# Value products of a half step in one block instead of two, with four buffers of turned probabilities

## The chip, the cores and the metric

The kernel runs on one NeuronCore of a Trainium2 chip. The metric is the device time of one launch in microseconds (us), median of the runs.

## The reference, cut to what matters

Two transformer layers on x of shape (64, 128, 256): 64 sequences of 128 tokens, width 256, float32. Each layer is a cross attention to a context of the same shape, then a mixture of experts. The change touches the two cross attentions only:

```
# layer 0: dilated attention; with 128 tokens per sequence its three branches are causal softmax
# attentions over all, every second and every fourth token, mixed by their log-sum-exp
x = x + L0_xattn(layernorm(x), ctx, ctx)
x = x + L0_ffn(layernorm(x))            # attention and MLP, each a mixture of 8 experts
# layer 1: plain causal attention
q, k, v = (n @ Wq + bq), (ctx @ Wk + bk), (ctx @ Wv + bv)      # 16 heads of 16
scores  = q k^T / 4, masked above the diagonal
x = x + softmax(scores) v @ Wo + bo
x = x + L1_ffn(layernorm(x))            # 8 experts, the best one of each token
```

## The kernel before

The program is a chain of stages: set-up, attention of layer 0 (its first scores begin 37 us into the span), the attention and the MLP of mixtures of layer 0, attention of layer 1 (from 2245 to 2790 us), routed experts. Both attentions are one function, `attention` (L270), called twice. The three branches of layer 0 become one softmax: what differs is added to the scores as a mask.

**Tiling.** The 64 sequences go two by two: 32 pairs per attention. A pair has two half steps, one for each sequence (s = 0, 1). In a half step the 16 heads are four units of four heads. A unit's scores, 128 queries by 4 x 128 keys, fill one PSUM bank (banks 0 to 3). So there are 64 half steps in each attention, 128 in all. `pairs` (L325) writes out the first 10 pairs (layer 0) or 2 pairs (layer 1) and the last 4, and runs the ones between in a hardware loop of two pairs per turn: 18 pairs in layer 0 and 26 in layer 1.

**One unit's way.** TensorE writes mask and scores of all four units at once (`score`, L419: 8 mask matmuls at L428, 16 products at L437). VectorE takes the row maximum of each unit (`row_max`, L632). ScalarE takes the exponentials, head by head, with their sums (`exps`, L555; lines L562). TensorE turns the unit's four probability matrices (`turn_p`, L442; transposes at L447) into bank 4 (units 0, 2, 3) or bank 0 (unit 1). VectorE copies them to SBUF, into `probsT` (`keep_p`, L638; copy at L642). TensorE multiplies them with the values (`times_v`, L450; L460, four column strips of the array at a time) into bank 5. The inverse of the sums is made and spread (`invert` on VectorE, `spread` on GpSimd), turned into the other half of bank 5 (`turn_recip`, L464), and `keep_o` (L650) copies bank 5 out.

**Order.** Each engine's order is written out by hand in its own `step`; the engines meet through semaphores that count. TensorE's half step is: score, turn unit 3 of the half step before, project the next pair's values (s = 0) or keys (s = 1), `times_v` of units 2 and 3 of the half step before, turn unit 0, `turn_recip`, project queries (s = 0) or the output (s = 1), turn units 1 and 2, with s = 0 turn the normalized x (`turn_n`, L370), `times_v` of units 0 and 1. VectorE's is: row maximum 0, keep unit 3 of before, row maxima 1 to 3, keep unit 0, keep_o, with s = 0 `keep_v` (L619), keep units 1 and 2, with s = 1 `residual`, `invert`, and with s = 0 `stats` and `rest_n` (L615). In the first pairs of layer 0 VectorE also measures x (`measure`, L727) between them. ScalarE's is four times `exps`, then with s = 0 `keep_q` and `round_n` (L537), with s = 1 `keep_k`, `norm` and, at the next pair's start, `round_c`.

**Waits that matter here.** `probsT` has two buffers, unit k uses k % 2: so `keep_p(k)` waits until `times_v(k - 2)` is done (`pv_done`, L641). The first mask matmul of `score` waits until unit 1's turned probabilities have left bank 0 (`pT_ready`, L427), and the mask matmul of unit u until the exponentials of unit u of the half step before are done (`exp_done`, L425). `rest_n` waits for `round_n`, and `project_k` for `rest_n` (`nlo_ready`, L382).

Of the kernel before, what the change touches and what calls it, by code (L numbers as in the profile page):

```python
# [26 lines left out]
P = 128  # L27
# [6 lines left out]
UH = 4  # L34
UNITS = H // UH
# [17 lines left out]
def wait(eng, sem, value):  # L53

    if isinstance(value, int) and value <= 0:
        return
    eng.wait_ge(sem, value)


def is_(index, value):  # L60

    return isinstance(index, int) and index == value
# [9 lines left out]
class Signals:  # L72
# [6 lines left out]
    def sem(self, name):  # L79
        self.all.append(self.stack.enter_context(self.nc.semaphore(name)))  # L80
        return self.all[-1]
# [188 lines left out]
def attention(nc, S, L, ctx_dram, W, bias, counted, load_next, signals, first, next_norms, next_table, x_dram=None):  # L270

    NP = S.n_seq // 2
# [3 lines left out]
    UP = 2 * UNITS  # L276
    rest_k16 = S.rest_count_k16 if counted else S.rest_k16
    with ExitStack() as mem:
        def sb(name, shape, dt=F32):
            return mem.enter_context(nc.sbuf_tensor(f"{L}_{name}", shape, dt))  # L280
# [8 lines left out]
        kT = sb("kT", [P, 2, KT, 2 * P])  # L289
        v_pad = sb("v_pad", [P, 2, 2, 2, 2 * UH, 32])  # L290
        probs = sb("probs", [P, UNITS, UH, P])
        probsT = sb("probsT", [P, 2, UH, P])
        neg_max = sb("neg_max", [P, UNITS, UH])
        sums, recip = sb("sums", [P, 2, KT, UH, 2]), sb("recip", [P, 2, KT, UH * 2])
        recip_wide = sb("recip_wide", [P, 2, KT, UH * 2 * D])
# [4 lines left out]
        pT_ps = [S.bank[n].rearrange("p (h k) -> p h k", h=UH) for n in (4, 0, 4, 4)]  # L300
# [14 lines left out]
        pT_made, pT_ready, pv_done, o_kept = sem("pT_made"), sem("pT_ready"), sem("pv_done"), sem("o_kept")  # L315
# [20 lines left out]
        with nc.Block() as block:  # L336
# [32 lines left out]
            def _(pe):  # L369
# [72 lines left out]
                def turn_p(p, k):  # L442
                    wait(pe, exp_done, UP * p + k + 1)
                    if k % UNITS != 1:
                        wait(pe, pT_ready, UP * p + k - (k % UNITS == 2))
                    for i in range(UH):
                        last = pe.transpose(pT_ps[k % UNITS][:, i, :], probs[:, k % UNITS, i, :], S.ident[:])  # L447
                    last.then_inc(pT_made, 1)

                def times_v(p, b, k):  # L450

                    s, u = divmod(k, UNITS)
                    m, e = divmod(u, 2)
                    wait(pe, pT_ready, UP * p + k + 1)
                    if u == 0:
                        wait(pe, o_kept, 2 * p + s)
                    if k == 0:
                        pe.wait_ge(v_ready, p + 1)
                    for i in range(UH):
                        last = pe.matmul(o_ps[32 * i:32 * (i + 1), 0, m, :], v_pad[:, b, s, e, UH * m + i, :],  # L460
                                         probsT[:, k % 2, i, :], start=u == 0, stop=True, skip_group_check=True)
                    last.then_inc(pv_done, 1)

                def turn_recip(p, s):  # L464
# [6 lines left out]
                def step(p, b):  # L471
                    for s in range(2):
                        before = (p, b, UNITS) if s else (p - 1, 1 - b, UP)
                        exists = s == 1 or not is_(p, 0)
                        score(p, b, s)
                        if exists:
                            turn_p(before[0], before[2] - 1)
                        if s == 0 and more(p, 1):
                            project_v(p + 1, 1 - b)
                        if s == 1 and more(p, 2):  # L480
                            project_k(p + 2, b)
                        if exists:
                            times_v(before[0], before[1], before[2] - 2)
                            times_v(before[0], before[1], before[2] - 1)
                        turn_p(p, UNITS * s)
                        if exists:
                            turn_recip(before[0], before[2] // UNITS - 1)
                        for half in range(2):
                            if s == 0 and more(p, 1):
                                project_q(p + 1, half)  # L490
                            if s == 1 and not is_(p, 0):
                                project_o(p - 1, half)
                        turn_p(p, UNITS * s + 1)
                        turn_p(p, UNITS * s + 2)
                        if s == 0 and more(p, 2):
                            turn_n(p + 2)
                        for u in range(2):
                            times_v(p, b, UNITS * s + u)

                turn_n(0)  # L500
                busy(pe, S, 8)
# [8 lines left out]
                project_k(1, 1)  # L510
                pairs(pe, step)
                turn_p(NP - 1, UP - 1)
                times_v(NP - 1, 1, UP - 2)
                times_v(NP - 1, 1, UP - 1)
                turn_recip(NP - 1, 1)
                for s in range(2):
                    project_o(NP - 1, s)
# [96 lines left out]
            def _(dve):  # L614
# [23 lines left out]
                def keep_p(p, k):  # L638

                    dve.wait_ge(pT_made, UP * p + k + 1)  # L640
                    wait(dve, pv_done, UP * p + k - 1)  # L641
                    dve.tensor_copy(probsT[:, k % 2], pT_ps[k % UNITS]).then_inc(pT_ready, 1)  # L642

                def invert(p, s):

# [1774 lines left out]
def program(nc, a, out):  # L2420

    with ExitStack() as mem:
# [66 lines left out]
        with ExitStack() as own:  # L2489
            W = Named()  # L2490
            W.hi, W.lo = weights(own, "W0", [P, 4, KT, C])
            signals = Signals(nc)
            attention(nc, S, "L0", a["ctx"], W, B["L0_xattn"], True, load_weights(1), signals, True, 2, ACT.Exp, a)
# [57 lines left out]
```

## Time and profile before

| | |
|---|---|
| median of 3 runs | 3059.33 us (3059.03 to 3063.7) |
| span of the profiled execution, first to last instruction | 3021.6 us |
| TensorE busy in it | 2857.8 us |
| VectorE busy in it | 2286.3 us |
| ScalarE busy in it | 1877.8 us |
| GpSimd busy in it | 1564.7 us |
| mean granted TensorE clock | 0.974 of full |

The profile is of one execution. It gives that execution's span and no other time of it; the span is 37.7 us under the median of the timed runs, which also holds what lies before the first and after the last instruction. Engines: PE is TensorE's matmuls, PEld its weight loads, DVE is VectorE, ACT is ScalarE, POOL is GpSimd. L460 is line 460 of the kernel. A time in brackets at the end of a row of the timeline is how long the engine sat idle before it, and behind the arrow what ended that ("issue": nothing that the profile shows).

### The profile page before, as it was taken

The page shows a single profiled execution, that of the slowest core. Times are in us where ns is not written, and L with a number is a line of the kernel's source. Part 1 is how long each engine was busy: PE and PEld are TensorE (multiplying, and loading weights), DVE is VectorE, ACT ScalarE, POOL GpSimd, SP SyncE. Part 2 cuts the span into 40 slices and gives each one's busy share as a digit, 9 for nine tenths or more (in the row PEclk, how much of TensorE's full clock was granted, in tenths as well). Part 3 has the DMA queues.
Part 4 walks back from the last instruction along what each step waited for, and adds up shares of the span by engine and source line. Part 5 has one row for each costly group of instructions (what it writes and reads, how often), then busy time and mean ns, then how long its engine had stood idle before and what let it go on. Part 6 is the DMA issues. An engine that isn't in the chain of part 4 may idle for free. (4 is left out here: it accounts for less than half of the span.)

```text
span 3021.6 us, 85335 instructions
## 1 busy us (share of the span) xinstructions
PE 2857.8 (95%) x26943; PEld 2563.3 (85%) x26944; DVE 2286.3 (76%) x6211; ACT 1877.8 (62%) x6970; POOL 1564.7 (52%) x1816
## 2 busy tenths in 40 slices
PE   6999999889999999997999999999989999998778
PEld 5878888689999999996999999999988888886556
DVE  6988888877777777776777777777768888888745
ACT  5888888755555555555344444444458888887735
POOL 3565656466666666665322222222226666654556
PEclk9999999999999999998999999999999999999779
DMA  6000000010000000000000000000010000000245
GB/s 222 16 19 15 17 14 14 2 62 11 10 10 10 10 11 12 10 10 25 25 11 10 10 10 10 10 10 10 5 47 18 17 14 14 17 14 2 93 140 150
DMA packets 56235, 86.43 MB, mean 29 GB/s; under 512 B 6944, under 2 KB 42785, under 8 KB 55458
## 3 DMA queue, kind: packets, MB, share of 16 engines
q1 hardware_dynamic: 49284, 66.47, 7.0%
q0 software_dynamic: 6528, 16.92, 1.5%
q8 instruction: 75, 1.23, 0.2%
q10 hardware_dynamic: 288, 1.31, 0.1%
q14 instruction: 60, 0.49, 0.1%
HBM read 57.25 MB, written 28.48 MB: 28 GB/s over the span
## 5 line engine op out<-in xcount | busy, mean ns | idle before, releaser
L562 ACT ACTIVATE L_probs<-bank,L_neg_max 128x128 f32<-128x128 f32 x2048 | 716.8, 403 | 150.4 <-DVE L_neg_max L636 149.9
L562 ACT ACTIVATION_READ_ACCUMULATOR L_probs<-bank,L_neg_max 128x1 f32 x2048 | 497.8, 243 | 0.0
L642 DVE COPY L_probsT<-bank 128x512 f32<-128x512 f32 x512 | 353.0, 689 | 136.6 <-PE bank L460 81.5
L1719 ACT ACTIVATE M_inter<-bank 128x512 f32<-128x512 f32 x256 | 153.3, 599 | 438.8 <-PE bank L69 387.9
L67 PE MATMUL bank<-W_hi,M_nT_hi 128*128 128x384 f32 (+1 forms) x1024 | 370.2, 362 | 8.3 <-DVE M_qkv L1345 4.4
L636 DVE TENSOR_REDUCE L_neg_max<-bank 128x4 f32<-128x512 f32 x512 | 327.6, 682 | 30.7 <-PE bank L437 30.6
L69 PE MATMUL bank<-W_lo,M_nT_hi 128*128 128x384 f32 (+1 forms) x1024 | 346.8, 339 | 0.0
L68 PE MATMUL bank<-W_hi,M_nT_lo 128*128 128x384 f32 (+1 forms) x1024 | 346.6, 338 | 0.0
L447 PE MATMUL bank<-constants,L_probs 128*128 128x128 f32 x2048 | 327.3, 284 | 12.9 <-ACT L_probs L562 10.1
L1778 DVE TENSOR_TENSOR M_inter_lo<-M_inter,M_inter_hi 128x512 fp32r<-128x512 f32 x256 | 207.1, 809 | 168.5 <-ACT M_inter_hi L1720 158.2
L67 PE MATMUL bank<-W_hi,M_inter_hi 128*128 128x256 f32 x1024 | 290.5, 284 | 11.8 <-DVE M_inter_lo L1778 11.0
L67 PE MATMUL bank<-M_nT_hi,W_hi 128*128 128x256 f32 x1024 | 296.8, 290 | 0.0
L447 PEld LDWEIGHTS bank<-constants,L_probs 128*128 128x128 f32 x2048 | 220.7, 141 | 82.7 <-ACT L_probs L562 66.6
L69 PE MATMUL bank<-M_nT_lo,W_hi 128*128 128x256 f32 x1024 | 290.4, 284 | 0.0
L68 PE MATMUL bank<-M_nT_hi,W_lo 128*128 128x256 f32 x1024 | 289.5, 283 | 0.0
L68 PE MATMUL bank<-W_hi,M_inter_lo 128*128 128x256 f32 x1024 | 287.7, 281 | 0.0
L69 PE MATMUL bank<-W_lo,M_inter_hi 128*128 128x256 f32 x1024 | 287.5, 281 | 0.0
L1875 POOL TENSOR_TENSOR M_gate_rnorm<-M_gate_squared,constants 128x2 f32<-128x2 f32 x32 | 24.4, 763 | 487.2 <-DVE M_gate_squared L1765 487.2
L818 POOL TENSOR_TENSOR L_o<-L_o_raw 128x256 f32<-128x256 f32 x128 | 93.3, 729 | 289.6 <-DVE L_o_raw L656 282.5
L67 PEld LDWEIGHTS bank<-W_hi,M_nT_hi 128*128 128x128 f32 x1024 | 193.6, 189 | 37.3 <-DVE M_qkv L1345 8.7
L1206 ACT ACTIVATE M_qkv_part<-bank,M_rw 128x384 f32<-128x384 f32 x192 | 111.5, 581 | 157.9 <-PE bank L69 157.8
L67 PEld LDWEIGHTS bank<-W_hi,M_inter_hi 128*128 128x128 f32 x1024 | 193.8, 189 | 18.2 <-issue 16.6
(334 smaller groups left out, 9144.7 us busy)
## 6 DMA issues: line engine op xcount, KB each, us to landing
L_ctx_in<-in_ctx SPq DMA_DIRECT2D x64, 256.0 KB, 2.6
M_tile<-M_sorted SPq DMA_DIRECT2D x72, 130.0 KB, 2.3
x_all<-in_x SPq DMA_DIRECT2D x8, 1024.0 KB, 10.5
raw_weights<-in_weights SPq DMA_DIRECT2D x2, 4096.0 KB, 15.6
hs<-M_hs SPq DMA_DIRECT2D x64, 128.0 KB, 1.7
M_hs<-hs SPq DMA_DIRECT2D x32, 256.0 KB, 2.6
M_sorted<-M_fill SPq DMA_DIRECT2D x16, 130.0 KB, 2.1
raw_weights<-in_weights SPq DMA_DIRECT2D x1, 2048.0 KB, 8.0
```

The source lines that it names most:

```text
L67: pe.matmul(out, left[0], right[0], start=first, stop=False)
L68: pe.matmul(out, left[1], right[0], start=False, stop=False)
L69: return pe.matmul(out, left[0], right[1], start=False, stop=last)
L447: last = pe.transpose(pT_ps[k % UNITS][:, i, :], probs[:, k % UNITS, i, :], S.ident[:])
L562: last = act.activation(probs[:, k % UNITS, i, :], score_bank[u][:, i, :], ACT.Exp, bias=neg_max[:, u, i:i + 1], scale=-1.0, accum_out=sum ...
L636: dve.tensor_reduce(neg_max[:, u, :], score_bank[u], AX.X, ALU.min).then_inc(max_ready, 1)
L642: dve.tensor_copy(probsT[:, k % 2], pT_ps[k % UNITS]).then_inc(pT_ready, 1)
L818: pool.tensor_tensor(o_sb[:], o_raw[:, s, 0, :], o_raw[:, s, 1, :], ALU.mult)
L1206: act.activation(qkv_part[:, e // 2 - 1, :], q_bank[1], ACT.Copy, scale=rw[:, b, 0, e:e + 1]).then_inc(M.odd_read, 1)
L1719: act.activation(inter[:, e % 2], up_bank[e % 2], ACT.Gelu).then_inc(M.inter_ready, 1)
L1778: dve.tensor_tensor(iT[1][:, e % 2].rearrange("p k t -> p (k t)"), inter[:, e % 2], iT[0][:, e % 2].rearrange("p k t -> p (k t)").bitcast( ...
L1875: pool.tensor_tensor(T.rnorm[:], T.squared[:], S.minus_half[:, 0:T.n], ALU.pow).then_inc(M.rooted, 1)
```

## The change

`probsT` gets four buffers instead of two, one for each unit. `times_v` of units 0 and 1 moves from the end of its half step into the block that already stands in the next one, so that this block holds units 0 to 3 in order. After the last pair it does so too. `keep_p(k)` waits for `times_v(k - 4)` instead of `times_v(k - 2)`. Number and shape of all instructions stay the same.

```diff
-        probsT = sb("probsT", [P, 2, UH, P])
+        probsT = sb("probsT", [P, UNITS, UH, P])
...
                         last = pe.matmul(o_ps[32 * i:32 * (i + 1), 0, m, :], v_pad[:, b, s, e, UH * m + i, :],
-                                         probsT[:, k % 2, i, :], start=u == 0, stop=True, skip_group_check=True)
+                                         probsT[:, u, i, :], start=u == 0, stop=True, skip_group_check=True)
...
                         if exists:
-                            times_v(before[0], before[1], before[2] - 2)
-                            times_v(before[0], before[1], before[2] - 1)
+                            for u in range(UNITS, 0, -1):
+                                times_v(before[0], before[1], before[2] - u)
                         turn_p(p, UNITS * s)
...
                         if s == 0 and more(p, 2):
                             turn_n(p + 2)
-                        for u in range(2):
-                            times_v(p, b, UNITS * s + u)
...
                 turn_p(NP - 1, UP - 1)
-                times_v(NP - 1, 1, UP - 2)
-                times_v(NP - 1, 1, UP - 1)
+                for u in range(UNITS, 0, -1):
+                    times_v(NP - 1, 1, UP - u)
...
                     dve.wait_ge(pT_made, UP * p + k + 1)
-                    wait(dve, pv_done, UP * p + k - 1)
-                    dve.tensor_copy(probsT[:, k % 2], pT_ps[k % UNITS]).then_inc(pT_ready, 1)
+                    wait(dve, pv_done, UP * p + k - UNITS + 1)
+                    dve.tensor_copy(probsT[:, k % UNITS], pT_ps[k % UNITS]).then_inc(pT_ready, 1)
```

## Rows read from the trace of the kernel before

**Rows 1.** The page: busy time, and the granted TensorE clock in 40 slices.
```profile
PE 2857.8 (95%) x26943; PEld 2563.3 (85%) x26944; DVE 2286.3 (76%) x6211; ACT 1877.8 (62%) x6970; POOL 1564.7 (52%) x1816
...
PEclk9999999999999999998999999999999999999779
```

**Rows 2.** Waits, whole span: waiter, cause, total us, times, longest.
```profile
DVE L_probsT L642 <- PE bank L460: 81.5, 128, 1.2
```

**Rows 3.** Timeline of ScalarE, one pair of layer 0's loop.
```profile
513.42 0.29 ACT L562 ACTIVATION_READ_ACCUMULATOR L_probs<-bank,L_neg_max 128x1 f32 x1
...
514.23 0.70 ACT L540 ACTIVATE L_nT_hi<-bank 128x512 fp32r<-128x512 f32 x1
516.64 0.37 ACT L562 ACTIVATE L_probs<-bank,L_neg_max 128x128 f32<-128x128 f32 x1 [1.71 <-DVE L_neg_max L636]
...
522.04 0.29 ACT L562 ACTIVATION_READ_ACCUMULATOR L_probs<-bank,L_neg_max 128x1 f32 x1
```

**Rows 4.** Timeline of VectorE, the same pair.
```profile
510.40 0.69 DVE L642 COPY L_probsT<-bank 128x512 f32<-128x512 f32 x1 [0.18 <-PE bank L447]
...
512.40 0.69 DVE L642 COPY L_probsT<-bank 128x512 f32<-128x512 f32 x1
513.96 0.69 DVE L642 COPY L_probsT<-bank 128x512 f32<-128x512 f32 x1 [0.87 <-PE bank L460]
...
514.73 0.69 DVE L670 BATCH_NORM_STATS2 stats<-x_all  x2
515.33 0.68 DVE L617 TENSOR_TENSOR L_nT_lo<-bank,L_nT_hi 128x512 fp32r<-128x512 f32 x1
515.92 0.68 DVE L636 TENSOR_REDUCE L_neg_max<-bank 128x4 f32<-128x512 f32 x1
```

**Rows 5.** Timeline of TensorE's weight loads, the same pair.
```profile
509.04 0.38 PEld L460 LDWEIGHTS bank<-L_probsT,L_v_pad 128*32 128x32 f32 x16
509.62 0.42 PEld L447 LDWEIGHTS bank<-constants,L_probs 128*128 128x128 f32 x4 [0.20 <-ACT L_probs L562]
...
511.66 0.46 PEld L447 LDWEIGHTS bank<-constants,L_probs 128*128 128x128 f32 x4
512.37 0.42 PEld L447 LDWEIGHTS bank<-constants,L_probs 128*128 128x128 f32 x4 [0.25 <-ACT L_probs L562]
...
513.39 0.38 PEld L460 LDWEIGHTS bank<-L_probsT,L_v_pad 128*32 128x32 f32 x16 [0.17 <-issue]
513.97 0.12 PEld L428 LDWEIGHTS bank<-constants 32*128 32x128 bf16 x8 [0.20 <-ACT L_probs L562]
...
516.12 0.19 PEld L67 LDWEIGHTS bank<-L_cT_hi,W_hi 128*128 128x128 f32 x1 [0.30 <-issue]
...
520.32 0.45 PEld L447 LDWEIGHTS bank<-constants,L_probs 128*128 128x128 f32 x4
```

**Rows 6.** Timeline of TensorE's matmuls, the same pair.
```profile
514.41 1.06 PE L437 MATMUL bank<-L_kT,L_q_half 32*128 32x128 f32 x32
```

**Rows 7.** Timeline of VectorE, first pair of layer 1.
```profile
2253.80 0.69 DVE L617 TENSOR_TENSOR L_nT_lo<-bank,L_nT_hi 128x512 fp32r<-128x512 f32 x1 [0.15 <-ACT L_nT_hi L540]
2254.41 0.68 DVE L636 TENSOR_REDUCE L_neg_max<-bank 128x4 f32<-128x512 f32 x1
```

**Rows 8.** Timeline of ScalarE, first pair of layer 1.
```profile
2252.26 0.30 ACT L562 ACTIVATION_READ_ACCUMULATOR L_probs<-bank,L_neg_max 128x1 f32 x1
```

**Rows 9.** Waits of the weight loads in 240 to 540 us.
```profile
PEld bank L428 <- issue: 6.0, 18, 0.5
```

**Rows 10.** Busy time by windows: length, busy by engine, granted clock, DMA.
```profile
53.36:60.19 6.83, 6.43 (x58) 4.67 (x62) 5.48 (x14) 6.47 (x30) 2.64 (x4) 0.50 0.10 38
...
240.00:540.00 300.00, 296.23 (x4138) 249.46 (x4140) 253.93 (x500) 263.63 (x1285) 181.21 (x231) 1.00 0.05 15
```

**Rows 11.** Timeline of VectorE, third pair of layer 0.
```profile
84.50 0.69 DVE L642 COPY L_probsT<-bank 128x512 f32<-128x512 f32 x1 [0.88 <-PE bank L460]
...
87.12 0.68 DVE L636 TENSOR_REDUCE L_neg_max<-bank 128x4 f32<-128x512 f32 x1
```

## The prediction, made before the changed kernel ran

> **What bounds the kernel now.** The page comes first. TensorE is busy 95% of the span [rows 1], so one would look for TensorE work that goes away. The change removes none; it only reorders. So the question is whether TensorE sets the pace in the two attentions, or a ring of waits through all engines does. The list of waits gives the lead: VectorE's copy of turned probabilities waits for a value product 128 times, once in every half step, 81.5 us in total [rows 2]. Whether that costs anything is read from the timelines of one pair.
>
> In them the last exponential of half step s = 0 ends at 513.42 + 0.29 = 513.71 and the first of the next half step starts at 516.64, after ScalarE sat idle for 1.71 us; it ends with the last one at 522.04 + 0.29 = 522.33 [rows 3]. From end to end that is 8.62 us: 2.93 from the last exponential to the first, 5.69 of exponentials. ScalarE waits in the first part, so what fills these 2.93 us is the bound. The first exponential follows row maximum 0, started at 515.92, by 0.72. That one stands at the end of a VectorE chain without any gap: copy of unit 2 at 513.96, reciprocal, statistics at 514.73, `rest_n` at 515.33, row maximum [rows 4]. The copy had been idle 0.87 us, and its releaser is `times_v` (L460). The scores themselves were not late: their first load is at 513.97 [rows 5] and their last product ends at 514.41 + 1.06 = 515.47 [rows 6], so a `score` takes 1.50 and was complete 0.45 before the row maximum begins. So in s = 0 the ring is: turn unit 2, `turn_n`, `times_v(0)` at 513.39 [rows 5], copy of unit 2, the VectorE chain, row maximum, exponentials. The wait for `times_v(k - 2)` is what the change takes away.
>
> In s = 1 the VectorE chain has no `stats` and no `rest_n`, and the next score is gated by the last exponential. There the ring has no `times_v` in it, save after the loop's branch (below).
>
> **The change, part by part.**
>
> *TensorE, s = 0.* The block of value products starts at 509.04 as before. With two units it took 0.58 to the next load, 509.62 [rows 5]. With four: at least 0.58 + 0.38 (the loads of two more units) = 0.96, at most two whole blocks, 1.16. I take 1.05. Unit 0 is then turned at 510.09 instead of 509.62 (its exponentials were done just before 509.62). From there to the turn of unit 1 are 2.04 us of matmuls (509.62 to 511.66 [rows 5]): 512.13. The turn of unit 2 then follows in 0.46 to 0.71 (the loads alone; 511.66 to 512.37, where 0.25 was waiting for ScalarE): 512.59 to 512.84. The 0.25 of waiting is the cover that takes up half of the delay. At the end of the half step 0.58 of value products (513.39 to 513.97) is gone.
>
> *VectorE, s = 0.* A copy starts about 0.78 after its turn starts (509.62 to 510.40 [rows 4, 5]). Unit 0: 510.87. Then `keep_o` and `keep_v` run as before, and the copy of unit 1 follows 2.00 later (510.40 to 512.40): 512.87. The copy of unit 2 no longer waits for a product; its turn allows it at 513.37 to 513.62 and VectorE is free at 512.87 + 0.61 = 513.48. So it starts between 513.48 and 513.62, instead of 513.96. What is late next? Reciprocal and statistics (0.77 from the copy to the statistics, 0.60 from these to `rest_n`) leave VectorE free for `rest_n` at 514.85 to 514.99. `rest_n` also needs `round_n` of ScalarE, which ends at 514.93 [rows 3]. This floor shows in the first pair of layer 1, where no statistics stand in the chain: `rest_n` starts at 2253.80, idle before it and released by ScalarE, 1.24 after the last exponential (2252.26 + 0.30), and the row maximum 0.61 later [rows 7, 8]. Here that gives `rest_n` at 514.96, row maximum at 515.57, first exponential at 516.29: 0.35 earlier than 516.64. The new limit is ScalarE's `round_n`, and the chain of VectorE beside it within 0.1.
>
> Score must not be late: it may now start when its first wait and the last exponential allow, about 513.71 + 0.05, and be complete at 515.27, 0.30 before the row maximum wants it. Its wait for the copy of unit 1 ends at 512.87 + 0.69 = 513.56. Behind that wait on TensorE stand only the scores.
>
> *s = 1.* `rest_n` ends 0.37 earlier, and `project_k` waits for it (516.12 [rows 5]), so it starts 0.37 earlier; the longer block costs 0.47; the turn of unit 1 is at 520.32 + 0.10 = 520.42, its copy at +0.74 = 521.16 to 521.85. The last exponential moves from 522.33 to 521.97. So score's first wait ends 0.1 before its last one: no loss, but no more than 0.1 of cover. Nothing is gained here in a plain half step. After the loop's branch there is something: of the 18 waits "issue" before score in 300 us, 6.0 us in all with a longest of 0.5 [rows 9], if nine are about 0.2, as the one before score in [rows 5], the other nine are 0.47 on average, one per turn of the loop. With the value products gone TensorE reaches the branch early. Bounds are 0 and 0.3 for each; I take 0.15.
>
> *Other queues.* `keep_o` comes about 0.5 later, and with it GpSimd's `normalize`; GpSimd is busy 181 of 300 us [rows 10], and its results are wanted in the next half step, so I cost it at nothing; without that cover it would cost what exceeds some 3 us. ScalarE and the DMA queues issue what they issued. After the last pair two more units (about 0.4 us) stand before the last product, but run while TensorE waits for the copy of unit 3 (0.69): nothing.
>
> *Sum.* Loop pairs: 18 + 26 = 44, times 0.35 = 15.4. Loop branches: 8 + 12 = 20, times 0.15 = 3.0. Pairs written out with the same chain (10th of layer 0, 29th and 30th of each attention): 5 x 0.35 = 1.8. Pairs 3 to 7 of layer 0: their chain from the copy of unit 2 to the row maximum has the measurements in it too, is unbroken and 2.62 long (84.50 to 87.12, 0.88 idle before it [rows 11]), so ScalarE's floor is not reached and the whole shift of the copy counts, 513.96 - 513.48 = 0.48: 5 x 0.48 = 2.4. Pairs 1, 2 and 8 of layer 0, same chain with other work: I take 0.4 each, 1.2. The first two and last two pairs of layer 1 and the last two of layer 0 have ScalarE's floor or a shorter chain: 0. Together 23.8 us. The profiled span would go from 3021.6 to 2997.8; the median is 37.7 above the span, which I keep: 3059.3 - 23.8 = 3035.5, say **3035**.
>
> **The rivals.**
>
> *A, part of it is given back.* The copies of units 1 and 2 come later than worked out, because the block or the two turns take longer. Each 0.1 beyond the 0.1 of cover costs 0.1 in s = 0 and as much in s = 1. With 0.2 too late in both: 64 x (0.1 + 0.1) = 13 of the 24, 3048. For it: the cover is thin in both half steps. Against: both are worked out with their upper ends (1.16, 0.71) and still hold nearly all.
>
> *B, no change.* The copy's idle time is no cause but a consequence, and the first exponential is held by something else to 2.93 after the last: 3059. For it: an engine that is busy 95%. Against: the pair of [rows 7, 8] has 2.57 there (0.72 more than 2254.41 - 2252.56), with the same scores and ScalarE work.
>
> *C, slower: score behind the copy of unit 1.* Today 0.58 of value products lie between the turns and score; they cover the copy out of bank 0. Without them score waits for it directly, with all matmuls behind it. Place: the first mask matmul. If the copy of unit 1 is late by L against the times above, s = 1 loses L - 0.1 and s = 0, whose copy of unit 2 follows it, changes by L - 0.48: slower from L of about 0.3. Priced at 0.7, one more VectorE operation before it: 64 x (0.6 + 0.2) = 51, less the 3 of the branches, 3107.
>
> *D, slower: the clock.* TensorE would now pause briefly before each score. The granted clock is 1.00 (2.4 GHz) in the loop with TensorE busy 296 of 300 us, and 0.50 (1.2 GHz) at 53 to 60 us, where the start-up left TensorE waiting [rows 10]. If half the length of that stretch, 3.4 us, ran at 1.2 GHz in each pair, its matmuls would take up to 1.7 us more: 64 x 1.7 = 109, 3144 with the gain. Against: pauses of 0.2 to 0.4 in 8.3 us are as long as those that the loop has already. The Trainium skill, "TensorE: Matmul & The Clock Gate", section "A second HAM failure mode: psum-queue depth-cycling", tells of a kernel whose short pauses between groups of matmuls made the clock go up and down; the loop's 1.00 shows nothing of it so far.
>
> *E, more: TensorE is the bound after all.* Then the change saves what stands around the moved block, the 0.17 before it and the 0.20 behind it [rows 5], in each half step: 128 x 0.37 = 47, 3012. The Trainium skill, "TensorEngine Tiling (Array Packing)", section "Key Properties", says that a change of tiling mode drains the engine, which would be these gaps; the trace agrees, as they stand where the array goes from whole to column strips and from these to row strips. Against: ScalarE is idle for 1.71 and TensorE waits for ScalarE (0.25) in the same half step.
>
> **How the numbers follow.** Forecast 0.70, A 0.12, B 0.08, C 0.04, D 0.03, E 0.03. What a measurement of this kernel tells from no change is about 0.2%, 6 us. Faster: forecast, A and E, 0.85. Same: B, 0.08. Slower: C and D, 0.07. Range: the forecast's terms with branches at 0.3 and chains at 0.40 give 20 x 0.3 + 49 x 0.40 + 3.6 = 29 us, 3030; with some to spare 3027. Upwards to A and a little beyond it, 3052; with B, C, D and most of E outside it leaves out somewhat under 2 in 10.
>
> **What would show it.** In the profile after: the waits of L642 for L460 gone; first exponential of s = 1 at 2.57 after the last one of s = 0, `rest_n` idle before it and released by L540; the block of L460 with 32 loads once per half step, turn of unit 0 about 1.05 after its start; the way from the last exponential of s = 1 to the first of s = 0 unchanged in plain half steps. Wrong, if the copy of unit 2 starts later than 0.12 before the last exponential ends, if score's first load comes after the last exponential of s = 1, or if the clock of the loops is under 0.98.

## The result, and the profile after

| | before | after |
|---|---|---|
| median of 4 runs | 3059.61 us (3059.03 to 3063.7) | 3036.01 us (3034.01 to 3038.49) |
| span of the profiled execution | 3021.6 us | 3031.9 us |
| time of that run | not given | 3034.01 us |
| attention of layer 0, layer 1 | 541.1, 528.2 us | 526.3, 516.4 us |
| last stage (routed experts) | 240.8 us | 276.4 us |
| the rest between the attentions | 1665.0 us | 1666.2 us |

The ratio is 0.9921, with a 95% interval of 0.9907 to 0.9934: 23.6 us faster, where 3035 was forecast. An attention is counted here from the last exponential of its first half step to that of its last one. The two together went from 1069.3 to 1042.6, 26.7 us less.

The two spans can't be compared as they stand: the profiled span after is longer, though the kernel is faster. No chip is on record for the profile and the times before, but two things say that they come from different ones: the last stage takes 235 to 242 us in every trace of one chip and 274 to 280 us in every trace of another, whichever kernel runs (the last section), and the kernel before takes 3025 us on the first and 3064 us on the second. The profile before is like the first in both, the times before are like the second. All comparisons of traces below leave that stage out.

First the waits, whole span, of after (waiter, cause, us in total, times, longest). `keep_p`'s copy is L640 now, two lines up.

```profile
ACT L_probs L560 <- DVE L_neg_max L634: 123.0, 120, 4.6
DVE L_probsT L640 <- PE bank L447: 108.6, 185, 1.1
PEld bank L428 <- ACT L_probs L560: 27.7, 76, 0.7
PEld bank L428 <- DVE L_probsT L640: 25.6, 44, 0.6
```

The wait for L460 [rows 2] is gone. ScalarE's wait for the row maximum is down from 149.9 to 123.0, by 26.9, about the gain in the attentions (26.7). VectorE's copies now wait for the turns instead (108.6 us against 49.8), which is not a loss by itself: they wait because they are early. TensorE's weight loads now pause before `score` (L428), for the exponentials or for the copy of unit 1.

One pair of layer 0's loop, as in [rows 3 to 5]. The weight loads of after:

```profile
495.31 0.81 PEld L460 LDWEIGHTS bank<-L_probsT,L_v_pad 128*32 128x32 f32 x32
496.32 0.42 PEld L447 LDWEIGHTS bank<-constants,L_probs 128*128 128x128 f32 x4 [0.20 <-issue]
...
498.37 0.90 PEld L447 LDWEIGHTS bank<-constants,L_probs 128*128 128x128 f32 x8
499.31 0.42 PEld L376 LDWEIGHTS bank<-constants,L_normed 128*128 128x128 f32 x4
500.00 0.24 PEld L428 LDWEIGHTS bank<-constants 32*128 32x128 bf16 x8 [0.28 <-ACT L_probs L560]
```

The block has 32 loads, and the turn of unit 0 starts 1.01 after it (estimate 1.05). The two turns of units 1 and 2 now stand without a gap, and `score` follows `turn_n` directly, 0.02 after the last exponential (next fence but one). VectorE:

```profile
497.11 0.69 DVE L640 COPY L_probsT<-bank 128x512 f32<-128x512 f32 x1 [0.62 <-PE bank L447]
...
499.20 1.29 DVE L640 COPY L_probsT<-bank 128x512 f32<-128x512 f32 x2
500.40 0.24 DVE L646 RECIPROCAL L_recip<-L_sums 128x16 f32<-128x16 f32 x1
500.56 0.69 DVE L668 BATCH_NORM_STATS2 stats<-x_all  x2
501.23 0.69 DVE L615 TENSOR_TENSOR L_nT_lo<-bank,L_nT_hi 128x512 fp32r<-128x512 f32 x1
501.84 0.68 DVE L634 TENSOR_REDUCE L_neg_max<-bank 128x4 f32<-128x512 f32 x1
```

The copies of units 1 and 2 are one run (x2, 0.6 apart), so unit 2's starts at 499.8, 0.18 before the last exponential ends; before, it started 0.25 after it. And ScalarE:

```profile
499.69 0.29 ACT L560 ACTIVATION_READ_ACCUMULATOR L_probs<-bank,L_neg_max 128x1 f32 x1
...
500.50 0.70 ACT L538 ACTIVATE L_nT_hi<-bank 128x512 fp32r<-128x512 f32 x1
502.56 0.37 ACT L560 ACTIVATE L_probs<-bank,L_neg_max 128x128 f32<-128x128 f32 x1 [1.36 <-DVE L_neg_max L634]
...
507.95 0.29 ACT L560 ACTIVATION_READ_ACCUMULATOR L_probs<-bank,L_neg_max 128x1 f32 x1
```

From last exponential to first it is 502.56 - 499.98 = 2.58 us, where it was 2.93 [rows 3], and from last to last 508.24 - 499.98 = 8.26, where it was 8.62. The clock, from the page, and a window in the loop of layer 0 (length, busy time by engine, granted clock, DMA):

```profile
PE 2831.6 (93%) x26944; PEld 2595.6 (86%) x26944; DVE 2283.2 (75%) x6211; ACT 1877.9 (62%) x6970; POOL 1563.8 (52%) x1816
...
PEclk9999999899999999997999999999999999998598
```

```profile
240.00:520.00 280.00, 272.81 (x3956) 246.96 (x3958) 243.19 (x479) 252.75 (x1231) 174.52 (x222) 1.00 0.05 15
```

The pauses before `score` left the granted clock at 1.00 (2.4 GHz). TensorE's busy share in the loop fell from 99% (296.23 of 300 [rows 10]) to 97% (272.81 of 280): its matmuls stand idle for 7.2 us before `score` in this window, 5.6 of them for the copy of unit 1 (16 times, 0.35 each). The kernel got faster with a less busy TensorE.

### The profile page after: what moved, and what is told of

It is laid out like the page before. It is cut to its first block and busy times, and to the rows that moved or that the text cites. A ratio compares the mean times of both kernels' runs of the same rounds, so it can differ in the third digit from the quotient of the medians.

```text
span 3031.9 us, 85376 instructions
## 1 busy us (share of the span) xinstructions
PE 2831.6 (93%) x26944; PEld 2595.6 (86%) x26944; DVE 2283.2 (75%) x6211; ACT 1877.9 (62%) x6970; POOL 1563.8 (52%) x1816
## 5 line engine op out<-in xcount | busy, mean ns | idle before, releaser
L560 ACT ACTIVATE L_probs<-bank,L_neg_max 128x128 f32<-128x128 f32 x2048 | 716.7, 402 | 123.9 <-DVE L_neg_max L634 123.0
L640 DVE COPY L_probsT<-bank 128x512 f32<-128x512 f32 x512 | 341.9, 687 | 110.3 <-PE bank L447 108.6
L447 PE MATMUL bank<-constants,L_probs 128*128 128x128 f32 x2048 | 304.5, 281 | 12.2 <-ACT L_probs L560 10.1
L447 PEld LDWEIGHTS bank<-constants,L_probs 128*128 128x128 f32 x2048 | 222.8, 141 | 57.5 <-issue 23.6
```

The costliest lines, as they stand in the source:

```text
L560: last = act.activation(probs[:, k % UNITS, i, :], score_bank[u][:, i, :], ACT.Exp, bias=neg_max[:, u, i:i + 1], scale=-1.0, accum_out=sum ...
L640: dve.tensor_copy(probsT[:, k % UNITS], pT_ps[k % UNITS]).then_inc(pT_ready, 1)
```

## The experiments

Two sets, each on one chip with its own runs of the kernel before: on the first its median was 3024.97 us (3021.51 to 3031.12, 17 runs), on the second 3063.84 us (3059.36 to 3072.05, 13 runs). Times across the sets are compared as ratios only. Periods (from the last exponential of one half step to that of the next) and the times after the last exponential of the half step before are medians over twenty pairs of layer 1's loop, unless a row is shown.

### e1_after_again: the changed kernel, no edit

> The changed kernel once more, for its loops and for the last stage. Open: in the two profiles the attentions became 26.7 us shorter, yet the span grew by 10.3, since the last stage (routed experts) took 35.6 us more after the change; the timed runs became 23.6 faster. Theory: the last stage varies from execution to execution, whatever the attentions do, and the profile of before caught a short one; then the ratio here is again 0.992 with its interval below 0.995, and the attentions' loop pairs take 16.43 us. Rival: the change lengthens the last stage; then the last stage stays above 270 us here in every execution and under 245 us in those of the kernel before.

Measured: 2996.64 us (2992.6 to 3003.59), ratio 0.9911 (0.9896 to 0.9926). The gain of the result came again, with 28.3 us in the medians and 23.9 in the attentions of the traces (1069.3 to 1045.4). The last stage takes 235.8 us with the changed kernel here, so the rival falls; what else it depends on is taken up in e5. This run is the reference for the next three.

### e2_buffers_only: four buffers, old order

From the kernel before:

```diff
-        probsT = sb("probsT", [P, 2, UH, P])
+        probsT = sb("probsT", [P, UNITS, UH, P])
...
-                                         probsT[:, k % 2, i, :], ...
+                                         probsT[:, u, i, :], ...
...
-                    wait(dve, pv_done, UP * p + k - 1)
-                    dve.tensor_copy(probsT[:, k % 2], pT_ps[k % UNITS])
+                    wait(dve, pv_done, UP * p + k - UNITS + 1)
+                    dve.tensor_copy(probsT[:, k % UNITS], pT_ps[k % UNITS])
```

> Four buffers of turned probabilities, with TensorE's order as before (value products of units 0 and 1 at the end of their half step). Theory: the gain comes from the copy of unit 2, which no longer waits for a value product, so that the next row maximum stands 1.86 after the last exponential instead of 2.21; score may be 0.3 later than in the changed kernel without harm. So half steps s = 1 of the loops take 8.26 as in the changed kernel, only the part of the branch is missing: about 19 to 21 us under the kernel before, 3040. Rival: the gain needs the block to move (TensorE's order, fewer changes of shape); then this one is within 6 us of the kernel before.

Measured: 3003.63 us (2995.58 to 3007.35), ratio 0.9926 (0.9912 to 0.9941). So 21.3 of the 28.3 us of e1 are there without any instruction having moved. The intervals of the two overlap; the attentions of the two traces are within 0.5 us of each other (1045.9 and 1045.4), while the last stage, which neither edit touches, takes 241.5 us here and 235.8 in e1. So the 7 us between the medians are no measure of the move. Weight loads, VectorE and ScalarE of one pair:

```profile
2567.94 0.38 PEld L460 LDWEIGHTS bank<-L_probsT,L_v_pad 128*32 128x32 f32 x16 [0.16 <-issue]
2568.51 0.12 PEld L428 LDWEIGHTS bank<-constants 32*128 32x128 bf16 x8 [0.20 <-ACT L_probs L562]
```

```profile
2566.99 1.40 DVE L642 COPY L_probsT<-bank 128x512 f32<-128x512 f32 x2
2570.12 0.68 DVE L636 TENSOR_REDUCE L_neg_max<-bank 128x4 f32<-128x512 f32 x1
```

```profile
2567.96 0.30 ACT L562 ACTIVATION_READ_ACCUMULATOR L_probs<-bank,L_neg_max 128x1 f32 x1
2570.84 0.37 ACT L562 ACTIVATE L_probs<-bank,L_neg_max 128x128 f32<-128x128 f32 x1 [1.36 <-DVE L_neg_max L636]
```

The value products still stand in front of `score`, which still starts 0.25 after the last exponential (2568.51 - 2568.26), as before. All the same the row maximum comes at 1.86 and the first exponential at 2.58, as in the changed kernel. So in s = 1 the copy's wait was the whole loss, and the late `score` none. What the move itself gives stands at the loop's branches: the two hardware loops took 742.0 us before (303.5 + 438.5), 727.1 here and 724.2 in e1. That is 14.9 us for the buffers (15.4 forecast) and 2.9 for the branches (3.0 forecast).

The move also costs something. Pairs 3 to 7 of layer 0 take 87.2 us before, 82.4 here and 84.6 in e1. There the chain from the copies to the row maximum sets the pace, and behind the longer block the copy of unit 0 starts 0.3 later: 2.97 before the last exponential ends in pair 5 of the result's trace, 3.27 here. So over both attentions the four buffers alone are as good as the whole change: most of the 2.9 us that the move gives at the branches is lost again in these five pairs (2.2).

### e3_two_blocks: the value products in two blocks of the next half step

From the changed kernel, in TensorE's step:

```diff
+                        if exists:
+                            for u in range(UNITS, UNITS - 2, -1):
+                                times_v(before[0], before[1], before[2] - u)
                         if s == 1 and more(p, 2):
                             project_k(p + 2, b)
                         if exists:
-                            for u in range(UNITS, 0, -1):
+                            for u in range(UNITS - 2, 0, -1):
                                 times_v(before[0], before[1], before[2] - u)
```

The same happens with s = 0 around the projection of the values. Nothing but TensorE's order changes.

> The changed kernel, but its block of four units is cut in two in the next half step: units 0 and 1 right after the turn of unit 3, units 2 and 3 after the projection. It puts one more change of array shape (about 0.2 us each way) back in each half step, 128 times, and leaves all waits alone. Theory: TensorE has slack in both half steps (about 0.2), and nearly all of it is used; loss against the changed kernel 0 to 10 us. Rival, TensorE is the bound: 0.37 x 128 = 47 us are lost, which is slower than before the change.

Measured: 3024.64 us (3019.75 to 3027.51), ratio 0.9994 (0.9985 to 1.0003). The whole gain is lost, far outside what I expected; the rival's size is nearer, but too large as well. Weight loads of one pair, then the first load of a `score` of s = 0, then ScalarE:

```profile
2584.72 0.38 PEld L460 LDWEIGHTS bank<-L_probsT,L_v_pad 128*32 128x32 f32 x16
2585.30 0.42 PEld L447 LDWEIGHTS bank<-constants,L_probs 128*128 128x128 f32 x4 [0.20 <-issue]
...
2588.98 0.24 PEld L428 LDWEIGHTS bank<-constants 32*128 32x128 bf16 x8 [0.28 <-ACT L_probs L563]
...
2591.12 0.38 PEld L460 LDWEIGHTS bank<-L_probsT,L_v_pad 128*32 128x32 f32 x16 [0.17 <-issue]
2591.70 0.19 PEld L67 LDWEIGHTS bank<-L_cT_hi,W_hi 128*128 128x128 f32 x1 [0.20 <-issue]
```

```profile
2563.49 0.20 PEld L428 LDWEIGHTS bank<-constants 32*128 32x128 bf16 x8 [0.58 <-DVE L_probsT L643]
```

```profile
2588.35 0.30 ACT L563 ACTIVATION_READ_ACCUMULATOR L_probs<-bank,L_neg_max 128x1 f32 x1
2591.45 0.37 ACT L563 ACTIVATE L_probs<-bank,L_neg_max 128x128 f32<-128x128 f32 x1 [1.58 <-DVE L_neg_max L637]
```

Each block stands between a gap of 0.13 to 0.17 and one of 0.20. One more block in each half step is 2 x (0.33 to 0.37) = 0.66 to 0.74 us more on TensorE in a pair. The periods grew from 8.18 and 8.28 (e1) to 8.45 and 8.49, by 0.48 together. So TensorE had about 0.2 of room in a pair, 0.1 in a half step, and all beyond it is paid in full. `score` now starts 0.33 after the last exponential (2588.98 - 2588.65), and the first exponential follows at 2.80. The changed kernel was thus close to a second bound, TensorE's own sequence, which is the thin cover that the prediction named in both half steps; I had taken it for thicker when I wrote this expectation. In s = 0 it is not TensorE alone: `score` starts 0.23 after the last exponential (2563.49 - 2563.26), when the copy of unit 1 lets it (the single row above), so that the bound there is TensorE up to the turn of unit 1 and then its copy, rival C's wait. With the copy's wait gone, the gaps of one more block at this place are no longer free. (e2 has two groups per half step as well, but its second one stands directly before `score`, which it makes 0.25 late in s = 1 without making the row maximum late.)

### e4_floor: the two things that hold `rest_n`, earlier

From the changed kernel. ScalarE splits x before it keeps the queries, and VectorE's statistics go before the copies of units 0 to 2:

```diff
# ScalarE's step, s == 0
+                        round_n(p + 2)
                         keep_q(p + 1)
-                        round_n(p + 2)
# VectorE's step
+                        if s == 0 and not (is_(p, 0) or is_(p, 1)):
+                            stats(p - 2)
                         keep_p(p, UNITS * s)
...
                         invert(p, s)
-                        if s == 0 and not (is_(p, 0) or is_(p, 1)):
-                            stats(p - 2)
```

> The changed kernel with the floor that was named as the new limit taken away: ScalarE rounds the next pair's normalized x before it keeps the queries, and VectorE takes the statistics of x ahead of the copy of unit 0, where it has been idle, instead of between the copy of unit 2 and the row maximum. Theory: the row maximum of s = 1 then follows the scores at about 1.60 after the last exponential instead of 1.86, half steps s = 1 take 8.00 to 8.05 instead of 8.26, 64 x 0.21 to 0.26 = 13 to 17 us under the changed kernel, 3020 to 3023. Rival: TensorE is the limit by now (its score is complete at 1.55 to 1.70); then half of that, 3028 or so, or nothing.

Measured: 2986.53 us (2986.17 to 2986.81), ratio 0.9872 (0.9857 to 0.9886), 10.1 us under e1. Weight loads, VectorE and ScalarE of one pair:

```profile
2559.18 0.24 PEld L428 LDWEIGHTS bank<-constants 32*128 32x128 bf16 x8 [0.26 <-issue]
```

```profile
2560.85 0.69 DVE L634 TENSOR_REDUCE L_neg_max<-bank 128x4 f32<-128x512 f32 x1 [0.25 <-PE bank L437]
```

```profile
2558.90 0.30 ACT L560 ACTIVATION_READ_ACCUMULATOR L_probs<-bank,L_neg_max 128x1 f32 x1
2561.58 0.37 ACT L560 ACTIVATE L_probs<-bank,L_neg_max 128x128 f32<-128x128 f32 x1 [0.97 <-DVE L_neg_max L634]
```

The row maximum now waits for the scores (L437) instead of the VectorE chain, and the first exponential is at 2.38 instead of 2.57. So the floor was `rest_n`, as the theory says, and lifting it gives 0.19 in s = 1. The rest of the way to what I expected is lost to TensorE: `score` there is released by nothing that the profile shows, it just comes when TensorE gets to it, and s = 0 went from 8.18 to 8.23. So the loops gave 6.0 us (724.2 to 718.2), where 44 x 0.21 to 0.26 = 9 to 11 were expected. Another 4.0 came from the first ten pairs (166.1 to 162.0). The two moves were not tried apart, so the share of each is open. This is the fastest kernel of this set.

### e5_before_again: the kernel before, no edit

> The kernel before once more, for the spans of its executions and for its last stage. The first profile of the changed kernel had 276 us after the last exponential of layer 1, three later ones on another chip 236 to 242, among them one of the same changed kernel; the profile of before had 241. Theory: the last stage differs between chips, not between kernels, and only about 2 us lie around a span, so the 37.7 us that the prediction put around it were mostly that difference. Then span and time differ by about 2 here, and the last stage is within 5 us of that of the other kernels of this job. Rival: the time around the span is about 38 for this kernel.

Measured: 3063.43 us (3054.59 to 3068.91), ratio 1.000 (0.999 to 1.001). It gives a trace of the kernel before on the second chip: attentions 539.5 and 528.8 us, within 1.6 of the first trace, and a last stage of 274.4 instead of 240.8. The profiled run takes 3054.59 us for a span of 3052.6, so 2.0 us lie around the span and the rival's 38 falls. The last stages of e6, e7 and e8 take 277.9, 280.0 and 277.8 us, one of them 0.6 further off than the 5 us expected.

### e6_wait_order: ScalarE waits for the row maximum last

From the changed kernel, in `exps`; the other two waits (for the turned probabilities and for the inverse; the inverse is ready 0.36 us before the row maximum starts in both traces below) now stand ahead of it:

```diff
-                    act.wait_ge(max_ready, UP * p + k + 1)
...
+                    act.wait_ge(max_ready, UP * p + k + 1)
```

> The changed kernel, but ScalarE waits for the row maximum after its other waits, not ahead of them. Between the start of row maximum 0 and the first exponential lie 0.89 us in the loops with s = 0, and 0.72 elsewhere; if the 0.16 is ScalarE working out its later waits, it goes, and half steps s = 0 of the loops could fall from 8.17 to 8.01. Theory: TensorE's own ring (score, turn of unit 3, projection, block, two turns, projection) is about 8.1 long by now, so they fall by 0.03 to 0.07 only, 1 to 3 us in all. Rival: TensorE is not near its limit; 44 x 0.16 = 7 us.

Measured: 3035.55 us (3031.37 to 3038.84), ratio 0.9902 (0.9881 to 0.9923), which can't be told from 0.9911. The traces show more. Row maximum 0 and first exponential of one half step s = 0, first the changed kernel:

```profile
394.85 0.69 DVE L634 TENSOR_REDUCE L_neg_max<-bank 128x4 f32<-128x512 f32 x1 [0.35 <-PE bank L437]
```

```profile
395.73 0.37 ACT L560 ACTIVATE L_probs<-bank,L_neg_max 128x128 f32<-128x128 f32 x1 [0.25 <-DVE L_neg_max L634]
```

And with the edit:

```profile
396.22 0.69 DVE L634 TENSOR_REDUCE L_neg_max<-bank 128x4 f32<-128x512 f32 x1 [0.35 <-PE bank L437]
```

```profile
396.95 0.37 ACT L560 ACTIVATE L_probs<-bank,L_neg_max 128x128 f32<-128x128 f32 x1
```

From row maximum to exponential it is 0.88 in the one and 0.73 in the other. In s = 1 of the loops, where ScalarE has been idle for over a microsecond, it is 0.71 to 0.72 with either order. Nearness of the waits to the row maximum does not explain this, though: in pairs 29 and 30 of both attentions, which are written out, ScalarE is idle still more briefly in s = 0 (0.09 to 0.11 us, for 0.25 in the loops), yet the changed kernel has 0.72 to 0.73 there, and with the edit it is 0.80 to 0.82, in s = 1 as well. The period of s = 0 fell from 8.17 to 8.02; that of s = 1 rose from 8.26 to 8.34, since its `score` now starts 0.17 after the last exponential. A pair takes 16.36 where it took 16.43: half is given back, where TensorE comes later to `score`. The loops together went from 722.8 to 719.6 us, the written-out pairs from 319.8 to 325.1 (0.1 more in most of their half steps, and two falls of the clock, see below), so that the attentions as a whole are 2.1 us longer with the edit.

### e7_floor_and_order: e4 and e6 together

> The last two edits together: ScalarE's rounding ahead of the queries, statistics moved into VectorE's idle time, and the row maximum awaited last. Every wait off TensorE would then allow half steps of 8.00. Theory, TensorE's ring bounds: 8.10 to 8.15 in all loop half steps, 0 to 3 us under the kernel with the first two edits alone, that is 38 to 41 under the kernel before. Rival: 8.00 in all of them, 10 to 13 us under it.

Measured: 3027.02 us (3025.50 to 3029.94), ratio 0.9874 (0.9855 to 0.9893), where e4 alone had 0.9872. A pair takes 16.31 us here and 16.32 in e4. Two edits that shorten two different waits add up to what the better one gives: the sign of a common bound that neither touches. `score` of s = 1 starts 0.17 after the last exponential, where e4 had 0.01 to 0.02 before it; that of s = 0 still waits 0.58 for the copy of unit 1.

### e8_less_tensor_work: e7 with less for TensorE to do

The projections of the queries and of the output leave out one of the three products that make an accurate one (the low part of the weights or of the output times the high part); of twelve matmuls in each, four go:

```diff
-                        last = mm3(pe, q_ps[:, m, :], ...
+                        last = mm2(pe, q_ps[:, m, :], ...
...
-                        last = mm3(pe, y_ps[:, s, :], ...
+                        last = mm2(pe, y_ps[:, s, :], ...
```

> The kernel of the run before this one, with one of the three products of each projected query and output tile left out (the low-order term; 4 of 12 matmuls of 256 columns in each half step, 0.12 us each, 0.48 us). It leaves out part of the computation. Theory: TensorE bounds the loops now, so that with 0.48 less they fall to the floor of the other engines, 8.00 to 8.03: 10 to 18 us under the run before it. Rival: something else holds them at 8.15 (a copy, ScalarE); then this one takes as long.

Measured: 3018.92 us (3018.13 to 3021.54), ratio 0.9851 (0.9832 to 0.9869), 8.1 us under e7. The traces show 4.7 less in the attentions (1033.9 to 1029.3): 5.9 less in the loops and 1.3 more in the pairs written out. The rest lies in stages that the edit does not touch. Either figure is less than the 10 to 18 expected. TensorE is a bound of e7, then, but not all of it. In s = 0 the period is 8.02 (8.06 in e7), and the first load of `score` comes 0.48 before the last exponential ends. In s = 1 it is 8.16 (8.25 in e7), and the weight loads show another wait. The last row is from the matmuls:

```profile
2566.50 1.02 PEld L453 LDWEIGHTS bank<-constants,L_probs 128*128 128x128 f32 x8
2567.91 0.42 PEld L382 LDWEIGHTS bank<-constants,L_normed 128*128 128x128 f32 x4 [0.39 <-issue]
2568.51 0.24 PEld L434 LDWEIGHTS bank<-constants 32*128 32x128 bf16 x8 [0.18 <-ACT L_probs L566]
```

```profile
2567.94 0.63 PE L382 MATMUL bank<-constants,L_normed 128*128 128x128 f32 x4 [0.18 <-DVE L_v_pad L630]
```

```profile
2566.92 0.88 DVE L630 TENSOR_TENSOR L_v_pad<-bank,rows 128x128 f32<-128x128 f32 x4
```

`turn_n` (L382 here) sat 0.39 idle. In the code it waits for `keep_v`, whose four operations VectorE ends at about 2567.8, 0.1 before `turn_n` starts. For the loads the profile names "issue", for the matmuls behind them `keep_v` (L630). That this wait is what still holds s = 1 is argued; no kernel here moved `keep_v` to show it.

## Why the prediction was right

**The bound.** A ring of waits, not TensorE's busy share: shown by e2, which takes nothing from TensorE and gives 14.9 us in the loops. Rival B (no change) falls.

**The copy of unit 2** was to start 0.09 to 0.23 before the last exponential; it starts 0.18 before. Block to turn of unit 0: 1.01, for 1.05.

**The new floor.** First exponential at 2.58 for 2.57 to 2.58, row maximum at 1.86. The period of s = 1 went from 8.61 to 8.26, 0.35 as forecast; e4 shows that `rest_n` is what holds it. One sign that I named did not show: `rest_n` is not idle before it. ScalarE's `round_n` ends at 501.20 and VectorE's statistics at 501.25, and `rest_n` starts at 501.23, so the two are level. I had them within 0.1 of each other and took `round_n` as the later; it changes nothing in the sum, but it is why e4 moved both.

**The cover of `score`.** The way from s = 1 to s = 0 was to stay as it was, with 0.1 of cover, and in half steps without a branch it does (first exponential at 2.47 before and after). Before it TensorE now waits 0.58 for the copy of unit 1:

```profile
393.20 0.22 PEld L428 LDWEIGHTS bank<-constants 32*128 32x128 bf16 x8 [0.58 <-DVE L_probsT L640]
```

That is rival C's wait, at its place. It ends 0.06 before the last exponential (393.26), so it costs nothing here; a lateness of some 0.1 more would begin to be paid. Rival A, the same lateness in small, did not come either.

**The terms of the sum.** Both loops: 18.4 forecast; 19.2 measured by the result's trace, 17.8 by e1's. Last four pairs of both attentions: 1.4 forecast, 1.1 measured (each 65.22 to 64.68). First ten pairs of layer 0: 4.0 forecast, 6.4 measured (172.3 to 165.9), but only 4.2 between the two later traces (e5's 170.3 to e1's 166.1). The difference is not the change's. Half step s = 0 of pair 9 went from 9.27 to 8.00 in the result's traces, since in the profile before the granted clock fell to 0.50 (1.2 GHz) just ahead of it; in e5, the same kernel, it did not, and the half step took 8.02. Of the ten traces three have the fall, with 9.02 to 9.27 in this half step, and seven do not, with 8.00 to 8.10. The stretch in both (length, busy time by engine, granted clock, DMA):

```profile
179.70:183.00 3.30, 3.30 (x18) 3.30 (x17) 1.17 (x2) 3.30 (x21) 0.57 (x1) 0.50 0.01 2
```

```profile
179.70:183.00 3.30, 3.19 (x53) 2.45 (x55) 1.67 (x3) 3.30 (x19) 2.14 (x3) 1.00 0.01 2
```

Pair 2 has another such difference (9.67 and 8.83 in s = 0 of the two traces before, with the clock at 0.50 for 6.8 us in the one and 3.4 in the other). Without these two half steps the first ten pairs gave 4.9 us in either comparison, 0.9 more than forecast. Pairs 3 to 7 gave 0.54 each on average for 0.48 (2.7 for 2.4), pairs 1, 2 and 8 together 0.8 for 1.2. Pair 9 had been left out of the sum, though its s = 1 has the plain chain (8.61 to 8.26, 0.35). And pair 10 gave 0.76 in s = 0 (9.29 to 8.53; 9.25 to 8.49 in e5 and e1), where I had forecast nothing: the turn of the inverse there waits for GpSimd, first before, then after.

```profile
198.75 0.20 PEld L468 LDWEIGHTS bank<-constants,L_recip_wide 128*128 128x128 f32 x2 [1.45 <-POOL L_recip_wide L808]
```

```profile
193.16 0.20 PEld L468 LDWEIGHTS bank<-constants,L_recip_wide 128*128 128x128 f32 x2 [0.53 <-POOL L_recip_wide L806]
```

The prediction had put everything on GpSimd at nothing, which holds in the loop and not here.

Together 23.8 were forecast in the attentions, 26.7 measured (23.9 by e1 against the trace before, 22.9 by e1 against e5), and 23.6 in the medians. In e1's set the medians give 28.3. So the sum is right by its terms, but that it hit the measured median to 1 us is partly luck.

**The account around the span was wrong.** I took 37.7 us to lie around the profiled span. In every run since, a profiled run's time is 2 us above its own span (3034.01 and 3031.9 after). Most of the rest is the last stage of the profile before, which is 34 us shorter than in e5. Only the difference of 23.8 went into the forecast, so the error cancelled. In a change to the last stage it need not have.

**The clock** (rival D) stayed at 1.00 in the loop, where the rival wanted 0.50 for part of each pair. Pauses of 0.28 and 0.58 us before `score`, one in each half step on the weight loads and 0.35 of the second on the matmuls, did nothing to it. The Trainium skill, "TensorE: Matmul & The Clock Gate", section "A second HAM failure mode: psum-queue depth-cycling", warns of short pauses between groups of matmuls; the loop does not bear that out for pauses like these. Where the clock did fall in an attention, in pair 9 above, TensorE had waited 2.44 and 0.78 us shortly before, in the trace with the fall and in e5 without it. e2 and e6 have a fall there too; e1, e4, e6, e7 and e8 have one in the last pair of an attention (1.0 us in e1); the result's trace after, e3 and e5 have none behind the first two pairs. So a single trace can be off by 1 to 2 us at such a place, with either kernel.

**Rival E** (TensorE is the bound, 47 us) was wrong for the kernel before, but half right for the one after: e3, e6, e7 and e8 show TensorE, with the copy of unit 1 behind it in s = 0, within about 0.1 us of setting the pace of a half step. The gaps on which it was priced are real, up to 0.17 before a block and 0.20 behind it, and e3 pays for most of them once they are doubled. The Trainium skill, "TensorEngine Tiling (Array Packing)", section "Key Properties", says that a change of tiling mode drains the engine; the trace agrees as far as the place of these gaps goes.

## What to carry to other kernels

An engine that is busy 95% of the span need not be the bound: look for a wait that occurs once in every step (128 times here), follow what comes behind it without a gap to the start of the next step, and take as gain only the way to the next floor, which some step of the same kernel often already shows. When a change has two parts, try each alone: here the buffers gave the gain, and what the moved block added in one place it took back in another. When a wait goes, ask at once which engine is level with the new floor: here three were (VectorE's chain, ScalarE's split, TensorE within 0.1 us), so that the later edits gave about half of what was expected of them in the loops. And look up whether the profiled run and the timed runs are alike stage by stage before their difference is called time around the span. A term read from one trace of pairs that occur once should be compared in a second trace of the same kernel.

## What the runs showed of the hardware

**The last stage depends on the chip.** Windows from the last exponential to the end (length, busy time by engine, granted clock, DMA share, GB/s); the changed kernel in the result and in e1, then the kernel before in e5:

```profile
2755.50:3031.90 276.40, 196.75 (x1118) 141.48 (x1118) 132.95 (x385) 130.20 (x293) 137.97 (x142) 0.78 0.34 105
```

```profile
2757.90:2993.80 235.90, 178.07 (x1117) 130.31 (x1118) 133.88 (x385) 129.74 (x293) 138.80 (x142) 0.84 0.40 123
```

```profile
2778.20:3052.60 274.40, 196.57 (x1102) 141.28 (x1102) 133.51 (x385) 131.19 (x293) 138.10 (x142) 0.77 0.34 105
```

The same work takes 235 to 242 us on one chip (four traces) and 274 to 280 on the other (four traces), with either kernel; the two traces of the result fit one group each. The attentions agree within 3 us. It is the stage that moves the most data, and TensorE's mean clock is lower in it where it takes longer. VectorE, ScalarE and GpSimd are busy for the same time on both. Whether slower transfers come first and the clock follows from TensorE's waiting, or something else, no run here tells.

**Gaps around the strips.** A group of value products stands between 0.13 to 0.17 us before and 0.20 behind it, whether 16 or 32 loads long. **The order of ScalarE's waits** is worth 0.15 us between row maximum and exponential in s = 0 of the loops (0.88 and 0.73) and nothing in s = 1 (0.71 and 0.72); in the pairs written out it costs 0.08 instead (0.72 without the edit, 0.80 with it) in both. What makes it so, no run here tells.
